# Layer 2 of a graph network kernel: the weighting of the values reads its exponentials from PSUM instead of SBUF

## Chip, cores and metric

The kernel runs on one core of one Trainium2 chip. The metric is the device time of one execution in microseconds (us); lower is better. Engines are named as in the profile: PE is TensorE, PEld its weight loads, DVE is VectorE, ACT is ScalarE, POOL is GpSimd, SP is SyncE.

## What is computed

Four graph layers run one after the other on 6250 nodes with 64 features and 200000 edges, sorted by target. Layer 0 sums weighted neighbours, layer 1 is a two-head attention with edge features of width 5, layer 2 a two-head attention with edge features of width 32 and an MLP, layer 3 a spline convolution. The change is in layer 2, whose part that matters is

```python
q = (h @ Wq + bq).reshape(n, HEADS, C)          # HEADS = 2, C = 64
k = (h @ Wk + bk).reshape(n, HEADS, C)
v = (h @ Wv + bv).reshape(n, HEADS, C)
e = (edge_attr @ We).reshape(-1, HEADS, C)
alpha = jnp.sum(q[tgt] * (k[src] + e), axis=-1) / math.sqrt(C)
ex = jnp.exp(alpha - amax[tgt])                 # amax: segment max over the target's edges
den = jax.ops.segment_sum(ex, tgt, num_segments=n)
agg = jax.ops.segment_sum((ex / (den[tgt] + 1e-08))[:, :, None] * (v[src] + e), tgt, num_segments=n)
```

## The kernel before

The edges lie in 128 runs of 1568, one run per partition. `attention_sums` of layer 2 walks along the runs in 112 chunks of T = 14 edges per partition, four chunks (UNROLL) to a turn of the loop. The segment softmax is made online: a running maximum and a running weighted sum are carried along each run, so the sum over a node's edges is a scan in which the old sum is scaled by one exponential (`exp[:, 0]`) and the new value is weighted by another (`exp[:, 1]`).

What each engine does for a chunk c:

- POOL, `gather`: 14 indirect DMAs (line 1823), each of which fetches one row of h per partition by an index that lies in SBUF (`idx`). Before every second one it waits on `made_ready`, so that the gathers for chunk c+2 keep pace with PE's matmuls for chunk c. `rows` has four buffers.
- PE, `turn` and `make`: it transposes the 14 tiles of gathered rows (line 1847) in four parts, and multiplies each by the weights for keys and values (line 1858), 28 matmuls of 128x256 with their pairs in two PSUM banks `made`.
- ACT: it copies the transposed parts (`rows_t`, line 1883), copies the seven pairs of keys and values from PSUM to `kv` (line 1888), fills `hold` with the spread queries (`fill`, lines 1901 and 1902), makes the exponentials (line 1906), spreads `exp[:, 0]` to `scale` (line 1909), and copies the running sums out (line 1916). Its order is written by hand in `step`: exponentials of c, then the copies for c+2, with the last pairs of c+2 at the end.
- DVE, also in a handwritten order in its own `step`: `products` of chunk n = c+1 for head 0 (line 1993) when the last pair of keys and values is there, and its carry (line 1994); then it waits on `exp_ready` and does `weigh(c, 0)`, which is a copy of the carried sums (line 2000) and the weighting itself (line 2001); a drain; the scan `sums(c, 0)` (line 2006); the reduction of the products; the scan `hold_query(n, 1)` (line 1985); `weigh(c, 1)`, `products(n, 1)`, `sums(c, 1)`; then `hold_query(m, 0)` of m = c+2, which waits for ACT's fill, and `running_max(n)` (lines 2011 to 2016), whose last instruction lets ACT make the exponentials of n.
- SP: the loads of indices, attributes and spread queries, and the stores.

`kv` and `exp` are in SBUF. `hold` (3840 bytes a partition) and `data` (3900 bytes) are in PSUM and take two banks of 2048 bytes each; `weigh` writes `data`. In layer 0 the early weighting has the other placement: the weights are copied into PSUM (line 865) and read from there (line 868), from a bank that holds no part of its output.

Of the kernel before, what the change touches and what calls it, by code (L numbers as in the profile page):

```python
# [13 lines left out]
ALU = mybir.AluOpType  # L14
# [3 lines left out]
P = 128  # L18
N = 6250
E = 200000  # L20
C = 64
# [5 lines left out]
H = 2  # L27
# [9 lines left out]
V2 = C + 1  # L37
# [50 lines left out]
def wait(eng, sem, value):  # L88

    eng.wait_ge(sem, value)  # L90
    eng.nop(nofuse=True)  # L91
# [1641 lines left out]
def attention_sums(nc, a, sem, g, tail, head):  # L1733
# [3 lines left out]
    T, NC, W = T2, L // T2, H * V2  # L1737
    with ExitStack() as stack:
        s = Space(nc, stack)
# [11 lines left out]
        arg, exp = s.sb("l2_arg", [P, 2, H, T]), s.sb("l2_exp", [P, 2, H, T])  # L1751
# [1 line left out]
        run = s.sb("l2_run", [P, 2, H, V2, T + 1])  # L1753
        outb = s.sb("l2_out", [P, 2, T, W + H])
        turned, made = s.ps("l2_turned", [P, 2, 512]), s.ps("l2_made", [P, 2, 512])
        hold, data = s.ps("l2_hold", [P, C, T + 1]), s.ps("l2_data", [P, V2, T + 1])
        two = lambda n: [sem(f"l2_{n}{b}") for b in range(2)]
        four = lambda n: [sem(f"l2_{n}{b}") for b in range(UNROLL)]
        idx_in, attr_in, got, turned_last = four("idx_in"), four("attr_in"), four("got"), four("turned_last")
# [5 lines left out]
        def pair(c, j):  # L1765

            n = c.r * PAIRS + j
            return n % 2, c.g * (UNROLL * PAIRS // 2) + n // 2

        with nc.Block() as block:  # L1770
# [189 lines left out]
            @block.vector  # L1960
            def _(v):
                v.memset(kv_w[:], 0.0)
                v.drain().then_inc(set_up, 1)
                for r in range(UNROLL):
                    v.sem_inc(turned_last[r], 1)
                v.memset(rows[:, :, :, F2 - 1:F2], 1.0)
                v.memset(rows[:, :, :, F2:], 0.0)
                v.memset(kv[:, :, :, H:, C:], 1.0)
                v.memset(keep[:], 0.0)
                v.memset(fresh[:], -FAR)  # L1970
                v.memset(top[:], -FAR)
                v.memset(scale[:], 0.0)
                v.memset(run[:], 0.0)
                v.tensor_copy(carry[:].rearrange("p h c -> p (h c)"), head[:, 0:H * C])
                v.sem_inc(turned_read[1], 1)
                for b in range(2):
                    v.sem_inc(made_read[b], 1)
                    v.sem_inc(stored[b], 16)
                v.drain().then_inc(set_up, 1)
                v.wait_ge(turned_read[0], 1)  # L1980

                def hold_query(c, h):
                    wait(v, filled[h], c.at + 1)
                    held_ = hold[:].rearrange("p f t -> p (f t)")
                    v.tensor_tensor_scan(held_, keep[:, c.b].rearrange("p f t -> p (f t)"), held_, 0.0, ALU.mult, ALU.add)  # L1985

                def products(c, h):
                    if h == 0:
                        n, uses = pair(c, PAIRS - 1)
                        wait(v, made_read[n], uses + 2)  # L1990
                        n, uses = pair(c, PAIRS - 2)
                        wait(v, made_read[n], uses + 2)
                    v.tensor_tensor(prod[:, h], hold[:, :, 1:].rearrange("p f t -> p t f"), kv[:, c.r, :, h, 0:C], ALU.mult)  # L1993
                    v.tensor_copy(carry[:, h], hold[:, :, T]).then_inc(held[h], 1)

                def reduce(c, h):
                    v.tensor_reduce(score[:, h, 1:], prod[:, h], AX, ALU.add)

                def weigh(c, h):
                    v.tensor_copy(data[:, :, 0], run[:, 1 - c.b, h, :, T])  # L2000
                    v.tensor_tensor(data[:, :, 1:].rearrange("p f t -> p t f"), kv[:, c.r, :, H + h],
                                    exp[:, 1, h].unsqueeze(2).to_broadcast([P, T, V2]), ALU.mult)

                def sums(c, h):
                    wait(v, scale_ready[h], c.at + 1)
                    v.tensor_tensor_scan(run[:, c.b, h].rearrange("p f t -> p (f t)"), scale[:, h].rearrange("p f t -> p (f t)"),  # L2006
                                         data[:].rearrange("p f t -> p (f t)"), 0.0, ALU.mult, ALU.add).then_inc(scanned[h], 1)

                def running_max(c):
                    flat = lambda t: t.rearrange("p h t -> p (h t)")  # L2010
                    v.tensor_tensor_scan(flat(top[:, c.b]), flat(fresh[:, c.b]), flat(score[:]), -FAR, ALU.add, ALU.max)
                    v.drain()
                    v.tensor_tensor(arg[:, 0], top[:, c.b, :, 0:T], fresh[:, c.b, :, 1:], ALU.add)
                    v.tensor_tensor(arg[:, 1], score[:, :, 1:], top[:, c.b, :, 1:], ALU.subtract)
                    v.drain()
                    v.tensor_tensor(arg[:, 0], arg[:, 0], top[:, c.b, :, 1:], ALU.subtract).then_inc(args_ready, 1)

                def step(c, n, m):
                    if n:
                        products(n, 0)  # L2020
                    if c:
                        wait(v, exp_ready, c.at + 1)
                        weigh(c, 0)
                    v.drain()
                    if c:
                        sums(c, 0)
                    if n:
                        reduce(n, 0)
                        v.drain()
                        hold_query(n, 1)  # L2030
                    if c:
                        if not n:
                            v.drain()
                        weigh(c, 1)
                    v.drain()
                    if n:
                        products(n, 1)
                    if c:
                        sums(c, 1)
                    v.drain()  # L2040
                    if n:
                        reduce(n, 1)
                        v.tensor_copy(score[:, :, 0:1], top[:, 1 - n.b, :, T:T + 1])
                        if m:
                            hold_query(m, 0)
                        v.drain()
                        running_max(n)

                def steps(g0):
                    at = [Chunk(g0, r) for r in range(UNROLL)] + [Chunk(g0 + 1, r) for r in range(2)]  # L2050
                    if isinstance(g0, int) and g0 == NC // UNROLL - 1:
                        at[UNROLL:] = [None, None]
                    for r in range(UNROLL):
                        step(at[r], at[r + 1], at[r + 2])

                hold_query(Chunk(0, 0), 0)
                v.drain()
                step(None, Chunk(0, 0), Chunk(0, 1))
                with v.Fori(0, NC // UNROLL - 1) as n:
                    steps(n)  # L2060
                steps(NC // UNROLL - 1)
                v.tensor_copy(tail[:, 0:W].rearrange("p (h f) -> p h f", h=H), run[:, 1, :, :, T])
                v.tensor_copy(tail[:, W:W + H], top[:, 1, :, T])
# [756 lines left out]
def layer2(nc, a, sem, g):  # L2820

    x = g["x"]
    ident = g["identity"]
    with ExitStack() as outer:
        s0 = Space(nc, outer)
        tail = s0.sb("l2_tail", [P, H * V2 + H])
        head = s0.sb("l2_head", [P, B2])

        source_sums_to_queries(nc, a, sem, g, head)
        g["clear_semaphores"]()  # L2830
        attention_sums(nc, a, sem, g, tail, head)

        target_sums_to_table(nc, a, sem, g, tail)
# [353 lines left out]
```

## Time and profile before

| | us |
|---|---|
| runs | 11424.32, 11443.05, 11444.75 (median 11443.05) |
| the profiled execution, its own time | 11473.53 |
| its span, first to last instruction | 11471.7 |
| mean granted TensorE clock over the span | 0.623 |
| layer 2's weighting, first to last | 6171.7 to 8727.2 |

The profiled execution took 30.5 us more than the median of the runs. The weighting's stage is about 22% of the span; the rest of the kernel isn't touched. Durations below are of this one execution.

### The profile page before, as it was taken

What the parts mean: (1) busy time and instruction counts of PE and PEld (TensorE: products, weight loads), DVE (VectorE), ACT (ScalarE), POOL (GpSimd) and SP (SyncE); (2) the same over time, 40 slices, a digit from 0 to 9 for tenths busy, and PEclk for the clock granted to TensorE, in tenths of its full rate; (3) what the DMA queues carried; (4) which work ended last, traced back from release to release, by engine and by line L of the source; (5) the groups of instructions that cost most, each with busy time, mean ns of one, the idle gap of its engine ahead of it and who ended that gap; (6) DMA issues with size and microseconds to landing.
All of it is one profiled execution on the core that took longest, in us unless ns stands there. A gap on an engine that the chain in (4) does not pass through costs nothing. (4 is left out here: it accounts for less than half of the span.)

```text
span 11471.7 us, 93591 instructions
## 1 busy us (share of the span) xinstructions
PE 3139.0 (27%) x19236; PEld 2584.7 (23%) x19236; DVE 6568.6 (57%) x9533; ACT 4808.3 (42%) x6902; POOL 6881.7 (60%) x6738
## 2 busy tenths in 40 slices
PE   1111588883000000000024555555554200000002
PEld 1111477773000000000023444444443100000001
DVE  6777666665211211119954767767675566666664
ACT  1111366662111111118954666666664434344332
POOL 5656555655677777764445555565553466666663
PEclk9999866765555555555556666666666655555555
DMA  3232322222232232226633444444441666666662
GB/s 91 89 83 78 66 70 71 71 78 32 104 108 91 104 107 91 103 80 248 260 123 87 113 109 110 115 109 115 108 111 55 195 200 204 199 205 204 199 200 79
DMA packets 722601, 1395.86 MB, mean 122 GB/s; under 512 B 409492, under 2 KB 439266, under 8 KB 714908
## 3 DMA queue, kind: packets, MB, share of 16 engines
q0 software_dynamic: 287072, 587.19, 19.2%
q1 hardware_dynamic: 406600, 639.22, 16.9%
q10 hardware_dynamic: 28852, 168.65, 4.0%
q14 instruction: 57, 0.47, 0.0%
q8 instruction: 20, 0.33, 0.0%
HBM read 827.38 MB, written 602.51 MB: 125 GB/s over the span
## 5 line engine op out<-in xcount | busy, mean ns | idle before, releaser
L828 POOL DMA_INDIRECT l_rows<-in_x,l_idx x1568 | 1563.1, 997 | 1084.7 <-issue 442.9
L1823 POOL DMA_INDIRECT l_rows<-h,l_idx x1568 | 1529.5, 975 | 1063.4 <-issue 424.5
L2904 POOL DMA_INDIRECT l_rows<-table,l_idx x1568 | 1487.3, 949 | 985.6 <-issue 525.0
L1352 POOL DMA_INDIRECT rows<-l_rows,l_idx x1568 | 1625.1, 1036 | 572.3 <-issue 544.2
L1858 PE MATMUL l_made<-l_kv_w,l_rows_t 128*128 128x256 f32 x3136 | 1145.1, 525 | 1183.7 <-ACT l_rows_t L1883 542.2
L1858 PEld LDWEIGHTS l_made<-l_kv_w,l_rows_t 128*128 128x128 f32 x3136 | 785.0, 267 | 1416.9 <-issue 1277.8
L2980 ACT ACTIVATE l_lifted<-l_rows,l_up 128x256 f32<-128x256 f32 x1568 | 653.1, 462 | 795.9 <-DVE l_half_low L2932 487.5
L1308 ACT COPY l_rows<-l_run 128x1792 f32<-128x1792 f32 x56 | 191.6, 3421 | 1730.8 <-POOLq L91 871.0
L2173 PE MATMUL l_small<-l_diag,l_ones 128*128 128x384 f32 x4 | 3.3, 927 | 3142.9 <-DVEq L2209 3142.9
L1341 DVE TENSOR_TENSOR l_rows<-l_run,l_weights_ps 128x56 f32<-128x56 f32 x56 | 12.0, 215 | 1466.2 <-issue 736.4
L1888 ACT COPY l_kv<-l_made 128x512 f32<-128x512 f32 x784 | 450.9, 595 | 658.4 <-DMA l_idx<-sorted_src 300.8
L2173 PEld LDWEIGHTS l_small<-l_diag,l_ones 128*128 128x128 f32 x4 | 1.0, 311 | 3143.8 <-DVEq L2209 3143.8
L1985 DVE TENSOR_TENSOR_SCAN l_hold<-l_keep,l_hold 128x960 f32<-128x960 f32 x224 | 484.1, 2161 | 328.6 <-issue 176.1
L255 DVE TENSOR_TENSOR r_hot_low<-l_iota_ps,r_low 128x896 bf16<-128x896 f32 x448 | 485.4, 1084 | 316.5 <-remote 274.8
L382 PE MATMUL r_rank<-r_before,r_low_tf 128*128 128x49 f32 x3136 | 660.9, 357 | 20.5 <-issue 19.8
L1066 PE MATMUL l_root_psa<-identity,x 128*64 128x128 f32 x49 | 12.9, 421 | 2322.5 <-DMA l_root<-in_root 2322.5
L382 PEld LDWEIGHTS r_rank<-r_before,r_low_tf 128*128 128x128 f32 x3136 | 631.6, 261 | 24.1 <-issue 23.8
L953 ACT COPY l_out<-l_run 128x448 f32<-128x448 f32 (+1 forms) x137 | 197.2, 1439 | 1038.4 <-DVE l_run L877 885.2
L2938 DVE SCALAR_TENSOR_TENSOR l_quarter<-l_half_high,l_up,l_half_low 128x128 f32<-128x128 f32 x1568 | 444.6, 352 | 167.7 <-issue 132.8
L1066 PEld LDWEIGHTS l_root_psa<-identity,x 128*64 128x64 f32 x49 | 9.0, 199 | 2324.2 <-DMA l_root<-in_root 2323.3
L2006 DVE TENSOR_TENSOR_SCAN l_run<-l_scale,l_data 128x975 f32<-128x975 f32 x224 | 488.4, 2180 | 16.1
L1993 DVE TENSOR_TENSOR l_prod<-l_hold,l_kv 128x896 f32<-128x896 f32 x224 | 244.6, 1092 | 429.7 <-ACT l_kv L1888 262.5
(423 smaller groups left out, 12597.1 us busy)
## 6 DMA issues: line engine op xcount, KB each, us to landing
sums<-l1s_out ACTq DMA_DIRECT2D x56, 1988.0 KB, 6.8
sums<-l_out SPq DMA_DIRECT2D x112, 924.0 KB
spread<-zeros SPq DMA_DIRECT2D x28, 3612.0 KB
l_spread<-spread SPq DMA_DIRECT2D x112, 903.0 KB
l1s_rows<-rows SPq DMA_DIRECT2D x56, 1008.0 KB, 6.2
spread<-zeros SPq DMA_DIRECT2D x56, 938.0 KB
l_spread<-spread SPq DMA_DIRECT2D x56, 938.0 KB
sums<-l_out ACTq DMA_DIRECT2D x56, 896.0 KB
```

The source lines that it names most:

```text
L255: v.tensor_tensor(hot_low, iota_b[:].unsqueeze(1).to_broadcast([P, SB, P]), low[:, at].unsqueeze(2).to_broadcast([P, SB, P]), ALU.is_equal)
L382: last = nc.tensor.matmul(self.rank[:, b, j, 0:NT], self.low_tf[:, r % HOT, j * P:(j + 1) * P], self.before[:, b, :, j], start=False, stop ...
L828: pool.indirect_dma_start(rows[:, b, t], None, a["x"], bass.IndirectOffsetOnAxis(ap=idx[:, b, t:t + 1], axis=0)) \
L1352: pool.indirect_dma_start(g["rows1_d"], bass.IndirectOffsetOnAxis(ap=idx[:, b, t:t + 1], axis=0), rows[:, b, t], None).then_inc(sent[b], 16)
L1823: pool.indirect_dma_start(rows[:, c.r, t, 0:C], None, g["h2_d"], bass.IndirectOffsetOnAxis(ap=idx[:, c.r, t:t + 1], axis=0)).then_inc(got[ ...
L1858: last = nc.tensor.matmul(made[:, n, j * 256:(j + 1) * 256], rows_t[:, q % 2, at:at + P], kv_w[:], start=True, stop=True)
L1888: nc.scalar.copy(kv[:, c.r, 2 * j:2 * j + 2, :, 0:C], made[:, n].rearrange("p (j s c) -> p j s c", j=2, s=2 * H)).then_inc(made_read[n], 1)
L1985: v.tensor_tensor_scan(held_, keep[:, c.b].rearrange("p f t -> p (f t)"), held_, 0.0, ALU.mult, ALU.add)
L2006: v.tensor_tensor_scan(run[:, c.b, h].rearrange("p f t -> p (f t)"), scale[:, h].rearrange("p f t -> p (f t)"), data[:].rearrange("p f t - ...
L2904: pool.indirect_dma_start(rows[:, b, t], None, g["table3_d"], bass.IndirectOffsetOnAxis(ap=idx[:, b, t:t + 1], axis=0)) \
L2938: v.scalar_tensor_tensor(out=quarter[:, j], in0=half_high[:, j], scalar=up[:, b, k * GROUP + j, 1:2], in1=half_low[:, j], op0=ALU.mult, op ...
L2980: last = nc.scalar.mul(lifted[:, n, j], rows[:, b, k * GROUP + j, 4 * C:], up[:, b, k * GROUP + j, 0:1])
```

## The change

`data` becomes a view of a tensor that fills both of its PSUM banks. The last 28 elements (2 heads x 14 edges) of the second bank, which `data` left free, become `share`. Once a chunk, DVE copies `exp[:, 1]` there and drains. Both heads' weightings read `share` in place of `exp`.

```diff
-        hold, data = s.ps("l2_hold", [P, C, T + 1]), s.ps("l2_data", [P, V2, T + 1])
+        hold, data_bank = s.ps("l2_hold", [P, C, T + 1]), s.ps("l2_data", [P, 1024])
+        data = data_bank[:, 0:V2 * (T + 1)].rearrange("p (f t) -> p f t", t=T + 1)
+        share = data_bank[:, 1024 - H * T:].rearrange("p (h t) -> p h t", h=H)
...
                 def weigh(c, h):
                     v.tensor_copy(data[:, :, 0], run[:, 1 - c.b, h, :, T])
                     v.tensor_tensor(data[:, :, 1:].rearrange("p f t -> p t f"), kv[:, c.r, :, H + h],
-                                    exp[:, 1, h].unsqueeze(2).to_broadcast([P, T, V2]), ALU.mult)
+                                    share[:, h].unsqueeze(2).to_broadcast([P, T, V2]), ALU.mult)
...
                     if c:
                         wait(v, exp_ready, c.at + 1)
+                        v.tensor_copy(share, exp[:, 1])
+                        v.drain()
                         weigh(c, 0)
```

## Rows read from the trace of the kernel before

**Rows 1.** The page's busy time, share of the span and instructions of each engine.

```profile
PE 3139.0 (27%) x19236; PEld 2584.7 (23%) x19236; DVE 6568.6 (57%) x9533; ACT 4808.3 (42%) x6902; POOL 6881.7 (60%) x6738
```

**Rows 2.** Busy time by window, layer 2's weighting stage: from:to, length, each engine.

```profile
6171.00:8728.00 2557.00, 1376.70 (x4612) 1073.17 (x4612) 1803.82 (x2113) 1635.22 (x2544) 1477.15 (x1517) 0.66 0.41 110
```

**Rows 3.** Waits in that stage: who, for whom, us in total, times, longest.

```profile
POOL l_rows L1823 <- PE l_made L1858: 422.0, 168, 6.8
ACT l_kv L1888 <- DMA l_idx<-sorted_src: 284.0, 66, 7.3
DVE l_prod L1993 <- ACT l_kv L1888: 262.5, 55, 8.4
...
DVE l_hold L1985 <- issue: 176.1, 84, 6.2
DVE l_prod L1993 <- issue: 157.3, 56, 6.5
...
DVE l_hold L1985 <- ACT l_hold L1902: 85.3, 29, 5.7
...
ACT l_exp L1906 <- DVE l_arg L2016: 8.4, 1, 8.4
```

**Rows 4.** The gathers' line 1823: duration min/median/max, and who waited for it.

```profile
L1823 POOL DMA_INDIRECT l_rows<-h,l_idx x1568: 942/947/4734, 6095.5 to 8669.3; - x196
...
  PE l_turned L1847: 22.6, 1
```

**Rows 5.** Groups of instructions, whole span: busy us, mean ns | idle before them.

```profile
L1823 POOL DMA_INDIRECT l_rows<-h,l_idx x1568 | 1529.5, 975 | 1063.4 <-issue 424.5 <-PE l_made L1858 422.3 <-DMA l_idx<-sorted_src 216.6
L2938 DVE SCALAR_TENSOR_TENSOR l_quarter<-l_half_high,l_up,l_half_low 128x128 f32<-128x128 f32 x1568 | 444.6, 352 | 167.7 <-issue 132.8
L2001 DVE TENSOR_TENSOR l_data<-l_kv,l_exp 128x910 f32<-128x910 f32 x224 | 247.5, 1105 | 0.0
L1993 DVE TENSOR_TENSOR l_prod<-l_hold,l_kv 128x896 f32<-128x896 f32 x224 | 244.6, 1092 | 429.7 <-ACT l_kv L1888 262.5 <-issue 158.8
L868 DVE TENSOR_TENSOR l_data_ps<-l_rows,l_iota_ps 128x1792 f32<-128x1792 f32 x28 | 56.8, 2029 | 33.2 <-DMA l_rows<-in_x,l_idx 31.8
L2951 DVE SCALAR_TENSOR_TENSOR l_data<-l_run,l_same,l_data 128x64 f32<-128x64 f32 x98 | 32.0, 327 | 82.8 <-issue 82.6
L865 DVE COPY l_iota_ps<-l_weight 128x28 f32 x28 | 5.0, 180 | 0.0
```

**Rows 6.** Timeline, DVE and POOL: start us, us taken, what, idle before.

```profile
6240.74 1.09 DVE L1993 TENSOR_TENSOR l_prod<-l_hold,l_kv 128x896 f32<-128x896 f32 x1 [4.27 <-issue]
6240.90 0.95 POOL L1823 DMA_INDIRECT l_rows<-h,l_idx  x1 [0.30 <-issue]
...
6242.05 1.10 DVE L2001 TENSOR_TENSOR l_data<-l_kv,l_exp 128x910 f32<-128x910 f32 x1
...
6242.15 1.82 POOL L1823 DMA_INDIRECT l_rows<-h,l_idx  x1 [0.31 <-issue]
```

**Rows 7.** Timeline of DVE over one of the shorter chunks.

```profile
7122.27 0.21 DVE L1994 COPY l_carry<-l_hold 128x64 f32<-128x64 f32 x1
7122.40 0.26 DVE L2000 COPY l_data<-l_run 128x65 f32<-128x65 f32 x1
...
7136.66 2.16 DVE L1985 TENSOR_TENSOR_SCAN l_hold<-l_keep,l_hold 128x960 f32<-128x960 f32 x1 [1.50 <-ACT l_hold L1902]
7138.90 0.22 DVE L2011 TENSOR_TENSOR_SCAN l_top<-l_fresh,l_score 128x30 f32<-128x30 f32 x1
7139.19 0.19 DVE L2013 TENSOR_TENSOR l_arg<-l_top,l_fresh 128x28 f32<-128x28 f32 x1
...
7141.46 1.09 DVE L1993 TENSOR_TENSOR l_prod<-l_hold,l_kv 128x896 f32<-128x896 f32 x1 [1.72 <-issue]
```

**Rows 8.** Windows from 6090 to 6830, gathers (line 1823), then ACT's copies (line 1883).

```profile
6090.00:6830.00 740.00, 436.22 (x448) 0.66 0.40 105
```

```profile
6090.00:6830.00 740.00, 61.76 (x121) 0.66 0.40 105
```

## Prediction

> **What bounds the kernel now.** The page comes first: over the whole kernel POOL is busy 60%, DVE 57%, ACT 42%, PE 27% [rows 1]. No engine is near full, so shares decide nothing, and the stage that the change touches has to be read by itself. Its window is 2557 us long, with DVE busy 1804, ACT 1635, POOL 1477 and PE 1377 [rows 2]: 22.8 us for each of the 112 chunks, of which DVE works 16.1, ACT 14.6 and POOL 13.2. A loop of engines that wait for each other sets this pace. The question is which of them the others really wait for, so the waits come next [rows 3]. DVE waits for ACT before its first products of a chunk 262.5 + 157.3 us in total, which is 3.7 us a chunk, and again before the scan of the queries, 176.1 + 85.3 us, 2.3 us a chunk. (The waits put down to "issue" stand at the same two instructions, behind the same semaphores; I count them as the same waits.) In the other direction ACT waits for DVE's last arguments once, 8.4 us. DVE is therefore a follower: what it does late within those 6 us a chunk costs nobody anything. POOL waits for PE's matmuls 168 times, 422 us. It is a follower too, and the line of the gathers says so from the other side: only PE ever waited for a gather, once, 22.6 us, when the stage began [rows 4]. How far ahead POOL is, two windows that end at 6830 show: 448 gathers have been issued, which are 32 chunks, while ACT has made 121 copies of transposed rows, four a chunk, so it has just begun the 31st [rows 8]. A chunk's rows lie there for a whole chunk before PE wants them. What is left is the round between PE and ACT: ACT's copies wait for matmuls (284.0 us under one label alone, which names a DMA, though the instruction's own semaphore is set by PE) [rows 3]. The change gives neither of them any instruction, and takes none.
>
> **The change part by part.** *The copy and its drain, once a chunk.* The trace has the twin of the copy: 28 elements from SBUF to PSUM, 180 ns (line 865) [rows 5]. A drain costs what lies between a short instruction's end and the next one's start: from 7138.90 + 0.22 to 7139.19, 0.07 us; without a drain the next one starts 0.08 us before the end (7122.27 + 0.21 against 7122.40) [rows 7]. The copy comes in behind the carry just as line 2000 did, so line 2000 is later by 0.18 + 0.07 = 0.25 us. Over 112 chunks that is 28 us of DVE's time. Queued behind it on DVE are the weighting, the scan of the sums, the reduction, the scan of the queries and so on to the running maximum. The first that somebody waits for are the copy-out of the sums, which ACT reaches late in its step, and the arguments of the exponentials. Ahead of those DVE itself waits, in one of the shorter chunks 1.50 us for ACT's fill, and after them 1.72 us for the keys and values, while ACT's exponentials stand in ACT's order right behind that same copy of keys and values [rows 7]. So 0.25 us goes into the first of these waits, and if it should be missing, into the second. On the path: nothing. Were both covers gone, the cost would be the 28 us. No wait on a semaphore is added, and SP's and POOL's queues are unchanged.
>
> *The weighting, 224 times, one source now in PSUM.* Two rows give the price of an element: (2029 - 1092) / (1792 - 896) = 1.046 ns, and what is left is fixed: 1105 - 952 = 153 ns for today's form (two sources in SBUF, result in PSUM), 155 ns for the form with one source in PSUM and the result in another PSUM bank (line 868), 155 ns for a PSUM source and an SBUF result (line 1993) [rows 5]. So the placement of the source costs about 2 ns, and 0.5 us in all, hidden as above. What none of these shows is a weighting that reads from the very bank that it writes: `share` and the second half of `data` lie together. The nearest row is an instruction of layer 3 which updates its PSUM operand in place: 327 ns for 64 elements, where a like one with separate banks takes 352 ns for 128, of which 352 - 134 = 218 is fixed. In place it has 327 - 67 - 218 = 42 ns over, 0.66 ns an element [rows 5]. Its other source is also strided, so this needn't be the bank. Bounds: nothing below, since no row has a TENSOR_TENSOR under 1.046 ns an element; above, one more step for each of 910 elements, 0.95 us. I take nothing for the sum: the broadcast operand changes once in 65 elements, and line 868 is the same operation. The row in between would give 0.60 us. Even at that, a chunk adds 0.25 + 1.20 = 1.45 us, which the 1.50 and 1.72 us still cover in turn.
>
> The Trainium skill speaks against the change here. "VectorE: DVE Perf Modes", section on the TRN2 errata, gives VectorE 120 cycles of fixed cost for a PSUM source against 58 for an SBUF source. By it each weighting would be some 65 ns longer, an estimate from the page's clock, 14.5 us in all, if exposed. Our rows of mixed sources differ by 2 ns and don't show it, and either amount is covered.
>
> *POOL is blocked no more.* A gather that starts inside line 1993 takes 0.95 us as ever; one that starts 0.10 us into line 2001 takes 1.82 us and ends 0.82 us after it [rows 6]. Line 2001 is the one long instruction here with two SBUF sources. The gathers' median is 947 ns and their mean 975: 28 ns x 1568 = 44 us, less 3.8 us for one gather of 4734 ns at the setup [rows 4, 5]. So POOL would get back about 40 us in the stage, 0.36 us a chunk. It is a whole chunk ahead [rows 8] and waits 422 us for PE already [rows 3]; the 40 us turn into a longer wait. On the path: nothing. Were POOL's cover gone, the gain would be 40 us.
>
> *Sum.* 0 + 0 + 0, and some 0.3 us at the end of the stage, where the last chunk has no cover: the profiled execution would go from 11473.5 to 11473.8. It lies 30.5 us over the median of the runs, so the forecast is 11443 us.
>
> **The rivals.** *Faster: the gathers' delays do reach the end.* For it: the block is real and repeated, and PE's hand-over to ACT shows irregular waits of up to 7.3 us [rows 3] whose cause no row names, so POOL's traffic may have a part in them. Against: nobody waits for a gather after the start. The whole of it gives 11473.5 - 40 - 30.5 = 11403 us. The Trainium skill has this mechanism in "SBUF — State Buffer", "Who interferes with whom": a VectorE instruction with two SBUF inputs contends with a GpSimd instruction that reads SBUF, and one with at most one doesn't. The trace agrees on the block, 1.82 us beside 0.95.
>
> *Slower: the weighting collides with itself in the bank.* The upper bound makes 0.25 + 2 x 0.95 = 2.15 us a chunk. It decides from about 1.7 us: where the first cover is missing, only the second's 1.72 us is there. All chunks so, 112 x 0.43 = 48 us: 11491 us. For it: the 42 ns of the in-place row. Against: most chunks have the first cover too.
>
> *The change doesn't do what it says.* POOL might be blocked by something else in line 2001, such as its strided writes into PSUM; then the gathers keep their 975 ns and the time is 11443 us all the same.
>
> *The round between PE and ACT shifts.* Granted clock is 0.66 in the stage [rows 2], between its levels of 1.2 and 2.4 GHz, and the hand-over waits are irregular. A small shift of when things start may move some of them: 25 to 30 us either way, from 10% of the 284 us, so 11415 or 11470.
>
> **How the numbers follow.** Within what a measurement can tell from no change, 0.2% or 23 us: the forecast with 0.50 and the change without effect on POOL with 0.06, together 0.56. POOL's gain, whole or in large part: 0.17. Bank collision: 0.10. A shift of the round: 0.08 faster, 0.09 slower. Faster 0.25, same 0.56, slower 0.19. The range starts at the faster rival, 11402, and stops at 11475, past the shift and short of the collision's upper bound, which leaves out some 0.15. The likeliest case by itself is 11425 to 11460.
>
> **What would show it.** Right: the copy near 180 ns x112; the weighting near 1107 ns; the gathers' mean down from 975 to about 950 with POOL's waits for PE longer by about 40 us; DVE's two waits shorter by some 28 us together; the stage still near 2557 us. Wrong: a weighting over 1.5 us (the bank), ACT waiting often for DVE's line 2016 (the cover was thinner), or a stage that is shorter by what the gathers gave up.

## The result, and the profile after

The changed kernel took 11500.9 us in the median of 13 runs (11468.77 to 11529.93), the kernel before 11425.19 us on the same chip (11384.44 to 11467.8, 13 runs). The ratio is 1.0071, with a 95% interval of 1.0058 to 1.0083: 0.7% slower, 76 us by the medians. The forecast was no change, and the time lies above its range. The two kernels are the same in all other stages. The profiled execution of before, 11473.53 us, happened to lie above all 13 runs of before, so the two traces differ by only 19 us (11492.32 against 11473.53 us), and what they show side by side is a quarter of the 76 us. A second profile of the changed kernel (e15 below) has a stage of 2582 us against 2575 in the first, and gathers of 948 ns in both.

What the prediction said of the added instructions holds. The page's groups for VectorE have the copy and the weighting (columns: count, busy us, mean ns, idle before):

```profile
L2003 DVE TENSOR_TENSOR l_data<-l_kv,l_data 128x910 f32<-128x910 f32 x224 | 246.4, 1100 | 0.0
L2025 DVE COPY l_data<-l_exp 128x28 f32<-128x28 f32 x112 | 20.2, 180 | 0.7 <-ACT l_exp L1908 0.7
```

The copy takes 180 ns, as its twin of layer 0 did, and the weighting 1100 ns against 1105 [rows 5], with a source in the very bank that it writes. So there is no collision in the bank. The gathers are unblocked too; first their line in the changed kernel's trace (minimum, median, maximum, first and last start), then their group:

```profile
L1825 POOL DMA_INDIRECT l_rows<-h,l_idx x1568: 942/947/4882, 6088.4 to 8686.2; - x196
```

```profile
L1825 POOL DMA_INDIRECT l_rows<-h,l_idx x1568 | 1487.1, 948 | 1129.5 <-PE l_made L1860 415.8 <-issue 414.9 <-DMA l_idx<-sorted_src 298.8
```

The mean fell from 975 to 948 ns [rows 5], which is 42 us of POOL's time, as foreseen. The stage by window in the changed kernel, with the columns of [rows 2]:

```profile
6169.00:8744.00 2575.00, 1346.94 (x4612) 1055.78 (x4612) 1819.34 (x2223) 1638.12 (x2542) 1432.09 (x1514) 0.67 0.40 109
```

VectorE works 15.5 us more (110 instructions more in these windows), POOL 45 us less, and the stage is 18 us longer all the same, with TensorE's granted clock at 0.67 against 0.66, so the clock isn't what it lost. The waits of the stage in the changed kernel (who, for whom, us in total, times, longest):

```profile
DVE l_prod L1995 <- ACT l_kv L1890: 503.3, 88, 8.4
ACT l_kv L1890 <- DMA l_idx<-sorted_src: 499.4, 114, 7.7
POOL l_rows L1825 <- PE l_made L1860: 415.8, 173, 6.7
...
POOL l_rows L1825 <- DMA l_idx<-sorted_src: 270.3, 114, 3.5
...
ACT l_kv L1890 <- PE l_made L1860: 191.2, 305, 2.0
ACT l_rows_t L1885 <- remote: 117.0, 43, 5.7
ACT l_kv L1890 <- issue: 97.1, 115, 3.8
DVE l_prod L1995 <- issue: 65.8, 22, 6.0
DVE l_hold L1987 <- ACT l_hold L1904: 55.5, 17, 5.4
DVE l_hold L1987 <- issue: 50.7, 48, 4.2
...
ACT l_rows_t L1885 <- PE l_turned L1849: 11.6, 45, 0.3
ACT l_rows_t L1885 <- issue: 1.2, 3, 0.5
ACT l_exp L1908 <- DVE l_arg L2018: 8.0, 1, 8.0
```

And the waits for TensorE in the kernel before that [rows 3] leaves out:

```profile
ACT l_rows_t L1883 <- remote: 245.3, 82, 5.5
ACT l_kv L1888 <- PE l_made L1858: 241.1, 315, 3.2
POOL l_rows L1823 <- DMA l_idx<-sorted_src: 190.3, 76, 3.9
...
ACT l_kv L1888 <- issue: 111.5, 112, 4.3
...
ACT l_rows_t L1883 <- issue: 10.3, 3, 5.0
ACT l_rows_t L1883 <- PE l_turned L1847: 9.3, 36, 0.3
```

Two readings. ACT waited for VectorE's arguments once, 8.0 us, against 8.4 before: VectorE is still the follower, and the copy is hidden. VectorE's own two waits for ACT, which the prediction wanted some 28 us shorter, went from 681.2 us (262.5 + 157.3 + 176.1 + 85.3) to 675.3, since their ends moved with ACT. And ACT's waits for TensorE are the account of the stage. (All of the lines for `l_kv` and `l_rows_t` are such waits, whatever name they bear: both instructions wait on semaphores that only TensorE's matmuls and transposes set.) For the keys and values they grew from 284.0 + 241.1 + 111.5 = 636.6 us to 499.4 + 191.2 + 97.1 = 787.7; for the transposed rows they fell from 264.9 to 129.8. Together 901.5 became 917.5, 16 of the stage's 18 us. So most of it is a shift: the long wait before the transposed rows, labelled "remote", came 82 times before and 43 after, and the one of up to 7.7 us that the profile puts down to a DMA, although the instruction's semaphore is TensorE's, 66 times before and 114 after. One of the latter, in the timeline of the changed kernel (start, us taken, what, idle before):

```profile
6904.77 2.05 PE L1860 MATMUL l_made<-l_kv_w,l_rows_t 128*128 128x256 f32 x4 [4.07 <-ACT l_kv L1890]
...
6906.60 1.91 PE L1849 MATMUL l_turned<-identity,l_rows 128*128 128x128 f32 x8
...
6908.88 0.94 POOL L1825 DMA_INDIRECT l_rows<-h,l_idx  x1 [0.30 <-issue]
6912.31 0.59 ACT L1890 COPY l_kv<-l_made 128x512 f32<-128x512 f32 x1 [6.53 <-DMA l_idx<-sorted_src]
6912.79 0.25 ACT L1908 ACTIVATE l_exp<-l_arg 128x56 f32<-128x56 f32 x1
6912.97 0.94 POOL L1825 DMA_INDIRECT l_rows<-h,l_idx  x1 [3.15 <-DMA l_idx<-sorted_src]
6913.06 1.09 DVE L1995 TENSOR_TENSOR l_prod<-l_hold,l_kv 128x896 f32<-128x896 f32 x1 [7.19 <-ACT l_kv L1890]
```

The matmuls of the last pair are over at 6906.82 by the record (6904.77 + 2.05), the transposes behind them at 6908.51, POOL's last gather at 6909.82, and ACT's copy of that pair starts at 6912.31. ACT and POOL, which wait on the same semaphore, are let go together, and for the 2.49 us before that no engine shows work. The ends of matmuls are modelled in the record, so TensorE might really have been at work so long. The trace's records of semaphore updates, which no view prints, speak against it: the last pair's comes at 6912.23, those of the two groups of transposes behind it at 6912.29 and 6912.35, though the second group alone took 0.85 us. The work was done, and word of it came late. I call this a late hand-over. When all wait for it, the chunk is longer by it.

### The profile page after: what moved, and what is told of

The parts are those of the page before. It is cut to its first block and busy times, and to the rows that moved or that the text cites. A ratio compares the mean times of both kernels' runs of the same rounds, so it can differ in the third digit from the quotient of the medians.

```text
span 11490.5 us, 93815 instructions
## 1 busy us (share of the span) xinstructions
PE 3107.1 (27%) x19236; PEld 2564.5 (22%) x19236; DVE 6585.6 (57%) x9645; ACT 4811.4 (42%) x6902; POOL 6831.6 (59%) x6738
## 3 DMA queue, kind: packets, MB, share of 16 engines
q0 software_dynamic: 287072, 587.19, 18.6%
## 5 line engine op out<-in xcount | busy, mean ns | idle before, releaser
L1825 POOL DMA_INDIRECT l_rows<-h,l_idx x1568 | 1487.1, 948 | 1129.5 <-PE l_made L1860 415.8
```

What stands on the lines that cost most here:

```text
L1825: pool.indirect_dma_start(rows[:, c.r, t, 0:C], None, g["h2_d"], bass.IndirectOffsetOnAxis(ap=idx[:, c.r, t:t + 1], axis=0)).then_inc(got[ ...
```

## The experiments

The theories at the start: (A) VectorE's added 0.25 us a chunk is on the path after all; (B) the unblocking of POOL's gathers shifts or multiplies the late hand-overs, either by the lockstep of gathers and pairs or by the gathers in flight. Sixteen kernels ran, in four groups on four chips, each beside the kernel before on the same chip. On three chips that one took 11411.91 (e1 to e4), 11454.58 (e5 to e8) and 11423.5 us (e13 to e16) in the median. On the fourth (e9 to e12) it took 9895.66 us, 13% less, which turned out to matter. "Stage" is the time from the first to the last weighting in a kernel's profiled execution, 2557 us for before and 2575 after.

| kernel | ratio, 95% interval | gathers' mean ns | stage us |
|---|---|---|---|
| changed kernel | 1.0071 [1.0058, 1.0083] | 948 | 2575 |
| e1 copy to SBUF instead | 0.9975 [0.9961, 0.9989] | 981 | 2491 |
| e2 ACT writes the share | 1.0069 [1.0049, 1.0089] | 948 | 2569 |
| e3 changed, POOL pauses | 1.0108 [1.0087, 1.0128] | 946 | 2634 |
| e4 before, gathers one pair later | 0.9891 [0.9871, 0.9911] | 977 | 2403 |
| e5 changed, gathers one pair later | 0.9934 [0.9916, 0.9953] | 945 | 2467 |
| e6 before, two pairs later | 1.0096 [1.0077, 1.0115] | 967 | 2632 |
| e7 before, one wait a chunk | 1.0015 [1.0000, 1.0030] | 981 | 2501 |
| e8 changed, one wait a chunk | 1.0117 [1.0096, 1.0138] | 948 | 2607 |
| e9 before, no gathers (9.9 ms chip) | 0.9990 [0.9981, 1.0000] | | 2087 |
| e10 changed, POOL pauses (9.9 ms chip) | 1.0353 [1.0339, 1.0367] | 947 | 2424 |
| e11 head 1 alone from PSUM (9.9 ms chip) | 1.0003 [0.9994, 1.0012] | 985 | 2083 |
| e12 head 0 alone from PSUM (9.9 ms chip) | 1.0001 [0.9992, 1.0010] | 978 | 2086 |
| e13 before, no gathers | 0.9611 [0.9574, 0.9649] | | 2086 |
| e14 changed, no gathers | 0.9599 [0.9561, 0.9638] | | 2086 |
| e15 changed kernel again | 1.0074 [1.0042, 1.0105] | 948 | 2582 |
| e16 e1 and e4 together | 0.9910 [0.9876, 0.9943] | 975 | 2421 |

One sum ties these stages together. Taken over each stage, ACT's waits for TensorE run from 427 us (e11) to 986 us (e6), and the stage less these waits is 1641 to 1665 us in every one of the 18 profiled executions. Whatever lengthened or shortened a stage did it through these waits.

### Is it VectorE's quarter of a microsecond, or what the PSUM source does? (e1, e2)

e1 keeps the copy and the drain, but into an SBUF tile, so the weighting has two SBUF sources as before. e2 drops them and lets ACT write the share into the PSUM bank itself.

```diff
 e1, against before
+        share = s.sb("l2_share", [P, H, T])
...
-                                    exp[:, 1, h].unsqueeze(2).to_broadcast([P, T, V2]), ALU.mult)
+                                    share[:, h].unsqueeze(2).to_broadcast([P, T, V2]), ALU.mult)
...
+                        v.tensor_copy(share[:], exp[:, 1])
+                        v.drain()
 e2, against the changed kernel
-                        v.tensor_copy(share, exp[:, 1])
-                        v.drain()
...
-                    nc.scalar.activation(exp[:], arg[:], ACT.Exp).then_inc(exp_ready, 1)
+                    nc.scalar.activation(exp[:, 0], arg[:, 0], ACT.Exp)
+                    nc.scalar.activation(share, arg[:, 1], ACT.Exp).then_inc(exp_ready, 1)
```

> Does all that the change adds to VectorE (the copy of the exponentials and the drain, once a chunk), but the copy goes to a tile in SBUF, so that the weighting has two SBUF sources as before. Theory A (the 0.25 us that VectorE gets a chunk are on the path after all): as slow as the changed kernel, ratio to before about 1.007. Theory B (the gathers, no longer blocked, run further ahead, and TensorE's last results of a chunk are then handed over late more often): ratio 1.000, gathers' mean still about 975 ns, and late hand-overs as often as before, some 48 in 108 chunks against 79.

> ScalarE writes the second set of exponentials straight into the free end of the bank, with an activation of its own; VectorE's copy and drain are gone. Theory A: VectorE has nothing to pay, but ScalarE has one more short instruction a chunk (about 0.25 us, 28 us in all if none is hidden), so 1.000 to 1.002. Theory B: the gathers are not blocked (mean about 948 ns), late hand-overs as often as in the changed kernel, ratio 1.007 or up to 1.009.

The copy alone costs nothing: e1 is 0.25% faster than before, so theory A is out. The PSUM source without the copy costs all of it: e2 is 0.69% slower. The gathers' group in the trace of e1, then in that of e2:

```profile
L1824 POOL DMA_INDIRECT l_rows<-h,l_idx x1568 | 1538.8, 981 | 989.8 <-issue 440.2 <-PE l_made L1859 334.1 <-DMA l_idx<-sorted_src 215.6
```

```profile
L1825 POOL DMA_INDIRECT l_rows<-h,l_idx x1568 | 1487.1, 948 | 1118.7 <-issue 418.4 <-PE l_made L1860 397.1 <-DMA l_idx<-sorted_src 303.3
```

Of these four kernels the slow ones have gathers of 948 ns, the others 981 or 975. Of the waits put down to a DMA, ACT has 243.8 us (61) in e1's stage and 482.9 us (115) in e2's. So the cost comes with the PSUM source and with the unblocking of POOL, which go together here. The cleanest pair is e1 and the changed kernel, which differ in no more than where the copy lies: 84 us of stage (2491 and 2575), of which 76 are ACT's waits for TensorE (841.2 and 917.5). Why e1 should beat before isn't explained by this.

### Can POOL be held back by other means? (e3)

```diff
 e3, against the changed kernel, before the 14 gathers of a chunk
+                    pool.memset(pace[:], 0.0)
+                    pool.drain()
```

> The changed kernel, with GpSimd held up once a chunk, ahead of its gathers, by a memset of 384 elements into a tile that nobody reads and a drain, some 0.4 us, about what the block took from it before. Theory A: nothing changes, ratio 1.007. Theory B: the gathers are less far ahead when TensorE makes the last pair, late hand-overs get rarer, ratio 1.000 to 1.004.

It came out at 1.0108, which neither theory had expected, and ACT's waits of the DMA's label rise to 603.6 us (133). But the pause didn't delay POOL. At this place POOL waits for TensorE's first pair anyway, and the pause lies inside that wait; POOL's timeline in e3:

```profile
7023.28 0.43 POOL L1822 MEMSET l_pace<- 128x384 f32 x1
7027.69 0.95 POOL L1828 DMA_INDIRECT l_rows<-h,l_idx  x1 [3.98 <-PE l_made L1863]
```

0.43 + 3.98 us lie between the last gather of one chunk and the first of the next, and in the changed kernel 4.40 us at 6919.56. In 107 of 110 chunks the first gather starts within 0.8 us of TensorE's semaphore, just as without the pause. So e3 doesn't test whether POOL is a fraction of a microsecond too early. Why a memset and a drain that move no gather cost another 0.4% stays open.

### Does the pace that couples the gathers to TensorE matter? (e4 to e8)

Before every second gather POOL waits for a pair of TensorE's two chunks back. e4 and e5 let it wait for one pair later, e6 for two, e7 and e8 only once a chunk.

```diff
 e4 against before, e5 against the changed kernel
-                            n, uses = pair(ahead_of, t // 2)
+                            n, uses = pair(ahead_of, min(t // 2 + 1, PAIRS - 1))
 e6 against before: min(t // 2 + 2, PAIRS - 1) there
 e7 against before, e8 against the changed kernel
-                        if ahead_of and t % 2 == 0:
-                            n, uses = pair(ahead_of, t // 2)
+                        if ahead_of and t == 0:
+                            n, uses = pair(ahead_of, 0)
```

> The kernel before, with the gathers held back by one more pair: the two gathers of pair p of chunk c+2 wait for TensorE's pair p+1 of chunk c (the last two pairs both wait for the last). Theory A: 1.000, the gathers are a chunk ahead anyway. Theory B: if it is their position that makes the hand-over late, this moves them back by 2.5 us at the time of the last pair, late hand-overs get rare and the kernel gets faster, ratio 0.985 to 0.995.

> The changed kernel with the gathers held back by one more pair, as in the run that took 0.989 without the change. Theory B1 (the change costs time through the step in which gathers and matmuls hold each other, pair by pair; the block used to break that step up): with the late step there is no late hand-over of the last pair, and the change costs nothing, 0.989 within 0.002. Theory B2 (unblocked gathers disturb TensorE wherever they stand): still 0.007 slower than without the change, 0.996.

> The kernel before with the gathers held back by two pairs. B1: the last pair's hand-over stays prompt, and less of the gathers' time falls beside the last pair; between 0.980 and 0.992, or a few tenths of a per cent slower than with one pair if the gathers of the end now come late. B2: no better than one pair, 0.989 or above.

> The kernel before, in which the gathers of a chunk wait for TensorE only once, for the first pair, and not pair by pair; the 14 then run in one go, 17.5 us. B1: the step is gone, GpSimd is through before the last pair in slow chunks; late hand-overs get rarer than 49 in 107, 0.985 to 1.000. B2: the same number of gathers in the same places, 1.000.

> The changed kernel with the same single wait a chunk. B1: without the pairwise step the change costs nothing, within 0.002 of the same edit without the change. B2: 0.007 slower than that.

When the gathers go out is worth more than the whole change: one pair later makes the kernel before 1.1% faster, two pairs later 1.0% slower (B1 had expected 0.980 to 0.992 for that, B2 0.989 or above). From the waits of e4's stage:

```profile
POOL l_rows L1823 <- PE l_made L1858: 280.6, 143, 7.9
ACT l_kv L1888 <- PE l_made L1858: 250.4, 264, 2.0
...
ACT l_kv L1888 <- DMA l_idx<-sorted_src: 133.9, 64, 6.1
```

Those 133.9 us were 284.0 [rows 3]. They have moved as well: 40 of before's 66 came at a chunk's last pair, and all but a few of e4's at the first, none at the last. In e6 they come at the first pair too, but in nearly every chunk (109 times, 392.0 us). TensorE waited for a gather once in each, when the stage began. Under each of three paces the unblocked form loses: 0.7% under the pace as it is, 0.4% one pair later (0.9934 / 0.9891 = 1.0043, two chips) and 1.0% with one wait a chunk (1.0117 / 1.0015 = 1.0102, one chip). So the loss isn't a trait of the lockstep of pairs: B1 expected none in e5 and e8. B2's 0.7% lies between the two.

### A chip without late hand-overs (e9 to e12)

e9 leaves out layer 2's gathers: their rows are a constant, and TensorE doesn't wait for them. e10 holds POOL before the ninth gather of a chunk. In e11 and e12 only one head's weighting reads PSUM.

```diff
 e9 (and e13), against before
-                        pool.indirect_dma_start(rows[:, c.r, t, 0:C], None, g["h2_d"],
-                                                ...).then_inc(got[c.r], 16)
...
-                        wait(pe, got[c.r], (c.g + 1) * (16 * T))
...
+                v.memset(rows[:, :, :, 0:C], 0.5)
 e10, against the changed kernel
+                        if t == 8:
+                            pool.memset(pace[:], 0.0)
+                            pool.drain()
 e11, against the changed kernel (e12: the other way round)
-                                    share[:, h].unsqueeze(2)
+                                    (share if h else exp[:, 1])[:, h].unsqueeze(2)
```

> The kernel before without layer 2's 1568 gathers: GpSimd keeps its waits on the indices and on TensorE's pairs but issues nothing, TensorE does not wait for gathered rows, and the rows hold a constant (so layer 2 computes on constants in place of the gathered features). If TensorE's late hand-overs need gathers in flight (theory B in its stronger form, B3), none is late here, and the stage goes from 2556 us to 2100 to 2300 us, 0.96 to 0.98 of the whole. If they have nothing to do with gathers, about 49 of 107 are late still and the ratio is 0.995 to 1.000.

> The changed kernel with GpSimd's pause (the memset of 384 elements, 0.44 us in the earlier run at the start of a chunk, and a drain) ahead of the ninth gather of a chunk instead. B3 (a pause in the stream of gathers lets TensorE's results through, and the block used to give such pauses): fewer late hand-overs than the 78 of the changed kernel, ratio 1.000 to 1.004. If only the total of GpSimd's time counts: as the pause at the start of the chunk, 1.011.

> The changed kernel, in which head 0's weighting reads the exponentials from SBUF as before, and only head 1's reads them from PSUM. One of the two blocks a chunk stays. Theory B: between the two kernels, and the two halves together give the 0.007 (less the 0.0025 that the copy and drain alone gained): 0.998 to 1.004. Theory A has nothing to say here any more.

> The complement: head 0 from PSUM, head 1 from SBUF as before. Theory B: 0.998 to 1.004; if one of the two blocks stands where it matters, one of these two runs is at 1.007 and the other at 0.998.

This chip ran the kernel before in 9895.66 us. There the stage takes 2083 us with all its gathers (in e11; before itself wasn't profiled on it), and leaving them out gains 0.1%, so e9 can't decide about late hand-overs: there are none to remove. ACT's waits in e11's stage show the difference:

```profile
ACT l_kv L1890 <- PE l_made L1860: 410.8, 544, 1.9
...
POOL l_rows L1825 <- PE l_made L1860: 83.0, 155, 1.6
...
ACT l_rows_t L1885 <- PE l_turned L1849: 15.6, 56, 0.9
```

None of the waits for TensorE of ACT or POOL bears a DMA's label, and none is above 1.9 us: no late hand-over. Which head is unblocked makes no difference, 0.03% and 0.01%. For the chips of 11.4 ms, e11 and e12 say nothing, since neither ran there. e10 was spoilt by its means. POOL's timeline in e10:

```profile
6012.45 0.43 POOL L1824 MEMSET l_pace<- 128x384 f32 x1
6017.08 0.95 POOL L1829 DMA_INDIRECT l_rows<-h,l_idx  x1 [4.20 <-issue]
```

The 0.43 us pause became 4.63 us with the drain, in the middle of a stream of gathers. TensorE then waited for rows, 733.6 us in the stage, and the kernel lost 3.5%. It is no test of a short pause.

### Does the lateness need the gathers, and is that all of the cost? (e13 to e16)

e13 is e9 again, on a chip of 11.4 ms; e14 leaves out the same gathers of the changed kernel; e15 is the changed kernel; e16 has the edits of e1 and e4.

> The kernel before without layer 2's 1568 gathers: the rows are filled with a constant once, and TensorE waits for no gather, so this part of the computation is left out. On a chip on which the kernel before takes about 11.4 ms: if TensorE's late results at a chunk's end come from gathers in flight, the stage shrinks towards the 21.4 us that a prompt chunk takes in the trace of before (112 chunks, some 2400 us) and the whole is 1 to 1.5% faster (ratio 0.985 to 0.990). If the late results have nothing to do with the gathers, the ratio stays within 0.998 to 1.002. On a chip on which before takes about 9.9 ms the earlier run gave 0.9990, and both theories expect that again.

> The changed kernel without layer 2's 1568 gathers, rows constant, the same part left out. If the change costs time only through its gathers, this equals the kernel before without gathers within 0.2%, whichever chip it is. If something else in the change costs time (VectorE's 0.25 us per chunk, or a read of the PSUM bank that is written), it is slower than that one by 0.3 to 0.8%.

> The changed kernel as it is. On a chip on which before takes about 11.4 ms: 1.006 to 1.008 as measured. On a chip on which before takes about 9.9 ms: the theory that the cost is TensorE's late hand-over, which no trace of such a chip shows, expects 0.999 to 1.001; a theory that the cost is in the change's own instructions expects 1.006 to 1.008 there too.

> The kernel before with the exponentials copied to an SBUF tile of their own and the gathers waiting for one pair later. The two edits gave 0.9975 and 0.9891 singly on chips of 11.4 ms. If they add up: 0.986 to 0.988. If both work on the same late results, and the later wait already takes them away: about 0.989. On a chip of 9.9 ms: 0.999 to 1.003.

Without its gathers the kernel before is 3.9% faster, far more than I expected. The windows of the stage in e13, then in e14:

```profile
6140.00:8226.00 2086.00, 1288.43 (x4612) 1022.08 (x4612) 1793.70 (x2111) 1636.13 (x2543) 0.00 (x0) 0.72 0.37 110
```

```profile
6141.00:8227.00 2086.00, 1287.46 (x4612) 1022.20 (x4612) 1814.49 (x2222) 1637.10 (x2542) 0.00 (x0) 0.72 0.37 111
```

And ACT's waits in e13's stage:

```profile
ACT l_kv L1885 <- PE l_made L1855: 416.7, 550, 2.0
ACT l_rows_t L1880 <- PE l_turned L1844: 14.5, 54, 0.3
```

Against before's trace the stage is 471 us shorter (2557 - 2086), and ACT waits 901.5 - 431.2 = 470 us less for TensorE; by the medians on this chip the kernel is 442 us faster. The late hand-overs are gone to the last one: a copy of a pair that ACT had waited for starts at most 0.39 us after the recorded end of its matmuls. The stage has the length that the chip of 9.9 ms gives it with gathers. So on the chips of 11.4 ms it is with the gathers that TensorE's hand-overs are late, for some 440 to 470 us a stage, although hardly anybody waits for a gathered row. The edit takes out three things at once: POOL's issuing, the transfers, and TensorE's wait for the rows (which are constant, too). On the chip of 9.9 ms the same edit gained 0.1%, so leaving out the wait and the data is worth nothing there. Whether the issuing or the transfers do the harm wasn't separated. And e14 equals e13: both stages are 2086 us, with VectorE 20.8 us busier in e14; the medians are 10967.95 and 10981.39 us, 0.12% apart, within both intervals. Whatever the change costs, it costs only with the gathers there. e15 repeats the loss on another chip (1.0074). e16 is no better than e4: the two faster edits work on the same waits.

## Why the prediction was wrong

The sum had three terms of nothing, and two of them were nothing. *The copy and its drain*: hidden, as worked out; e14 against e13 shows 112 of them at no cost, and e1 the same among gathers. *The weighting*: 5 ns less instead of 2 ns more, no collision with its own bank; that rival is out, and so is that the change doesn't do what it says. The Trainium skill ("VectorE: DVE Perf Modes", the TRN2 errata) led to an estimate of some 65 ns more for a PSUM source; the 1100 ns measured, against 1105, don't show it.

**The step that failed** is the third: "the 40 us turn into a longer wait. On the path: nothing." Its first half is right. POOL's waits for PE (both labels, since they are the same semaphore) went from 422.0 + 190.3 to 415.8 + 270.3 us, 74 us more, in a stage 18 us longer. The second half took it that an engine that nobody waits for can act on others by being late alone, and put this term at nothing. The runs show otherwise: the rows gathered a chunk ahead aren't missed by anybody, yet with the gathers there TensorE's results come late, 471 us of the stage in before's trace and none in e13, and the change costs 76 us with the gathers (by the medians) and nothing without them (e14 against e13). Line 2001 had held up POOL's gathers by 42 us in all, at most 0.87 us in one (1.82 - 0.95) [rows 6]. That the loss comes about because the gathers, no longer held up, fall otherwise against TensorE's pairs is argued and not shown. What the traces have is that the waits under the DMA's label, the longest among them, come 114 times instead of 66, and those before the transposed rows 43 times instead of 82.

**The rivals.** The last, that the round between PE and ACT shifts, had the mechanism in view, but was sized at 25 to 30 us, a tenth of one wait of 284 us. It measured 76 us by the medians. Its 10% was a guess, and the base too small: ACT's waits for TensorE were 901.5 us in all, of which 470 are irregular, as only 431 stay without gathers. The 76 us are 16% of those 470. The first rival, faster by 40 us, assumed that what the unblocked gathers gain would be passed on; the sign was wrong. The Trainium skill's rule beside it ("SBUF — State Buffer", "Who interferes with whom") agrees with the block: gathers of 981 ns in e1 and 948 in the changed kernel, which differ in no more than where the copy lies. It doesn't say that relief from it can cost more than the block.

**What stays open.** Shown is that the loss needs the gathers (e13, e14), comes with the PSUM source and not with the copy (e1, e2), and persists under three paces. Not shown is that the unblocking of POOL is the link between them, since every kernel on these chips that reads from PSUM also has the unblocked gathers, and none unblocks them otherwise. Nor is it shown how gathers make a hand-over late, or what ends one. In the changed kernel's timeline above, ACT is let go 2.49 us after POOL's last gather ended (6909.82 to 6912.31), and of 79 chunks whose last pair is copied over 1 us after its matmuls' recorded end, 48 are let go 2.3 to 3 us after such an end. Of the other 31, POOL is still in a gather in 6; in 25 it too has stopped and waits, for 0.02 to 2.14 us. Before had 14 of 48 of the first kind. So the end of the gathers doesn't set the moment by itself. e6 shows that holding the gathers back further makes it worse. Why e1 gains 0.25% is open as well, and the changed kernel itself wasn't run on the chip of 9.9 ms; only its halves were, at no cost.

The best version for the chips of 11.4 ms is e4, the kernel before with every pair of gathers waiting for one pair later: 0.9891 [0.9871, 0.9911].

## What to carry to other kernels

An engine that nobody waits for still has traffic in flight, and that can slow those on the path: before costing its speed-up at nothing, look whether the hand-overs of the engines that do set the pace are irregular, and let the range reach towards the whole of the irregular part (470 us here, of which 76 came). Where a wait's label names a DMA that has nothing to do with its semaphore, as `l_idx` here, take it as a question; one run without the suspected gathers says whether they matter at all. When transfers go out is a knob of its own: holding the gathers back by one pair of matmuls gained 1.1%, and one pair more lost that and 1.0% on top. And before using a pause as a test, look where the engine already waits: a pause inside such a wait delays nothing (e3).

## What the hardware showed that I hadn't expected

- A TENSOR_TENSOR that reads a broadcast source from the PSUM bank that it writes takes 1100 ns for 910 elements, against 1105 with that source in SBUF.
- ACT waited up to 7.7 us for a pair from TensorE with the gathers, and at most 2.0 us without them, on chips of 11.4 ms. In the changed kernel's trace the hand-over of a chunk's last pair came up to 6.4 us after the recorded end of its matmuls, in e13 at most 0.39 us. The pace of the stage, 22.8 us a chunk, is 18.6 without gathers.
- Chips differ: the kernel before took 9895.66 us on one and 11411.91 to 11454.58 on three. On the first the same gathers cost nothing in this stage. That is about 470 us of the 1500 between the chips; the rest lies in other stages and wasn't followed up. Layer 0's gathers waited less there too; their group in e11, then in e1, which is from a chip of 11.4 ms:

```profile
L828 POOL DMA_INDIRECT l_rows<-in_x,l_idx x1568 | 1621.6, 1034 | 602.0 <-issue 449.2 <-PE r_rank L313 87.5 <-DVEq L319 38.8
```

```profile
L828 POOL DMA_INDIRECT l_rows<-in_x,l_idx x1568 | 1564.1, 998 | 1071.6 <-issue 441.8 <-remote 254.0 <-PE r_rank L382 244.0
```

- A drain on POOL in a stream of gathers (e10) went with 4.20 us of idle time before the next gather, 4.2 in the median of 112, beside 0.30 between gathers without one.
